# An attention stage on one core: the last two features and the constant column of an outer product move from GpSimd to ScalarE

## The reference, cut to what matters

```python
def _L1_gnn_ref(feat, efeat, W_msg, b_msg, W_attn, b_attn, src, dst):
    w_m = (efeat @ W_msg + b_msg).reshape(E, in_f, -1)
    w_a = (efeat @ W_attn + b_attn).reshape(E, in_f, -1)
    h_src = feat[src][:, :, None]
    e1 = w_m * h_src
    e2 = w_a * h_src
    seg_max = jax.ops.segment_max(e2, dst, num_segments=N)
    ex = jnp.exp(e2 - seg_max[dst])
    denom = jax.ops.segment_sum(ex, dst, num_segments=N)
    attn = ex / denom[dst]
    ft = jax.ops.segment_sum(e1 * attn, dst, num_segments=N)
    return ft.sum(axis=1)
...
x = _layernorm(x + _L0_gnn_ref(x, edge_weight, src, dst), axis=-1)
x = _layernorm(x + _L1_gnn_ref(x, edge_attr_16, L1_gnn_W_msg, L1_gnn_b_msg, L1_gnn_W_attn, L1_gnn_b_attn, src, dst), axis=-1)
x = _layernorm(x + _L2_gnn_ref(x, edge_weight1, L2_gnn_W, L2_gnn_b, src, dst), axis=-1)
x = _layernorm(x + _L3_gnn_ref(x, edge_index, L3_gnn_eps1, ...), axis=-1)
```

## Time and profile before

| | |
|---|---|
| median of three runs | 8206.96 us (8204.55 to 8208.66) |
| the profiled execution | 8196.03 us, of which the traced span is 8194.2 us |
| share of the span: PE, DVE, ACT, POOL | 87%, 85%, 19%, 65% |
| the attention stage: first and last `outer` start | 1295.0 and 4452.2 us |
| granted TensorE clock over the whole span | 0.959 |

### The profile page before, as it was taken

The page is one execution under the profiler, slowest core; times in us unless marked ns, Lnnn a source line. Parts: engine busy times, 40 slices in busy tenths (PEclk is TensorE's granted clock), DMA queues, the critical chain, the costliest instruction groups (busy, mean ns, idle before and its releaser), DMA issues.

```text
span 8194.2 us, 205237 instructions
## 1 busy us (share of the span) xinstructions
PE 7100.0 (87%) x77871; PEld 6660.7 (81%) x77871; DVE 6989.1 (85%) x12224; ACT 1570.8 (19%) x3861; POOL 5336.9 (65%) x4570
## 2 busy tenths in 40 slices
PE   5999985888888988888887099999499997799994
PEld 5999975777777777777776099999499997799994
DVE  7999976999999999999999488888488886688884
ACT  0000002444444444444443200000000000000000
POOL 3555557888888888888886655555455555455554
PEclk9999998999999999999999599999799998899997
DMA  2222213555555455455554211111111111111110
GB/s 88 87 83 87 87 48 91 152 155 155 152 155 156 152 156 154 152 156 155 152 155 145 77 48 46 47 48 46 29 48 48 48 48 32 42 48 47 47 48 21
DMA packets 738221, 757.27 MB, mean 92 GB/s; under 512 B 153760, under 2 KB 698336, under 8 KB 738112
## 3 DMA queue, kind: packets, MB, share of 16 engines
q1 hardware_dynamic: 592640, 667.34, 24.7%
q0 software_dynamic: 140528, 86.77, 6.7%
q10 hardware_dynamic: 5008, 2.59, 0.1%
HBM read 239.80 MB, written 519.73 MB: 93 GB/s over the span
## 4 chain that ended last, share of the span: by engine, by line
PE 41%; DVE 30%; issue 23%; POOL 4%; DMA 1%; DVEq 1%; ACT 0%; ACTq 0%; POOLq 0%; SPq 0%; another core or an unknown queue 0%
PE ps L798 41%; DVE amax_room L1206 6%; DVE spare L1211 4%; DVE flat L1233 3%; DVE msg L1111 2%; DVE stt L928 2%; POOL got L451 2%; DVE flat L928 2%; DVE run L1132 1%; DVE spare L1215 1%; DVE raw L928 1%; DVE wide_buf L928 1%; DVE flat L1090 1%; DVE junk L1138 1%; POOL wide_buf L451 1%
## 5 line engine op out<-in xcount | busy, mean ns | idle before, releaser
L451 POOL DMA_INDIRECT msg<-feat,cidx x1680 | 1686.0, 1004 | 1580.9 <-PE ps L798 1172.2
L798 PE MATMUL ps<-parts,wide_buf 128*128 128x160 bf16 x30240 | 2123.2, 233 | 291.1 <-DVE wide_buf L1090 279.7
L798 PEld LDWEIGHTS ps<-parts,wide_buf 128*128 128x128 bf16 x30240 | 2100.2, 98 | 303.8 <-issue 283.7
L451 POOL DMA_INDIRECT hsrc<-feat,aidx x1568 | 1897.0, 1210 | 457.8 <-issue 327.8
L798 PE MATMUL ps<-parts,flat 128*128 128x160 bf16 x30240 | 2113.3, 233 | 25.7 <-DVE flat L1090 21.1
L798 PEld LDWEIGHTS ps<-parts,flat 128*128 128x128 bf16 x30240 | 2093.6, 98 | 33.1 <-DVE flat L1090 25.1
L845 PEld LDWEIGHTS ps<-wsb,zT 102*128 102x128 f32 x9408 | 1464.1, 190 | 222.9 <-ACT zT L684 201.2
L845 PE MATMUL ps<-wsb,zT 102*128 102x192 f32 (+1 forms) x9408 | 1543.3, 313 | 101.9 <-ACT zT L684 101.2
L1111 DVE TENSOR_REDUCE msg<-raw 128x288 f32<-128x2880 f32 x224 | 1130.4, 5046 | 7.8
L928 DVE TENSOR_TENSOR raw<-ps,amask 128x960 f32<-128x960 f32 x448 | 737.9, 1657 | 463.4 <-PE ps L798 351.0
L451 POOL DMA_INDIRECT msg<-in_x,cidx x560 | 561.3, 1002 | 553.5 <-PE ps L798 310.0
(11 more groups left out here) (218 smaller groups left out, 4681.3 us busy)
## 6 DMA issues: line engine op xcount, KB each, us to landing
state_tab<-flat SPq DMA_DIRECT2D x784, 512.0 KB
raw<-quot_tab SPq DMA_DIRECT2D x224, 576.0 KB
run_tab<-run SPq DMA_DIRECT2D x224, 224.0 KB
top_tab<-spare SPq DMA_DIRECT2D x392, 128.0 KB
msg<-feat,cidx POOLq DMA_INDIRECT x1680
hsrc<-feat,aidx POOLq DMA_INDIRECT x1568
efs<-in_ef SPq DMA_DIRECT2D x392, 34.0 KB
msg<-in_x,cidx POOLq DMA_INDIRECT x560
```

Of the source, the lines that this page charges most:

```text
L451: return pool.indirect_dma_start(dest, None, table, rows_at(idx))
L798: last = nc.tensor.matmul(block.rearrange("p (q c) -> p q c", c=D), hot[s][:, m, t * P:(t + 1) * P], parts[:, m * Q:(m + 1) * Q, part, :], ...
```

## The change

`outer` on GpSimd now makes 14 of the 16 source features (OI = 14) and 16 of the 17 columns: 4 x 14 x 16 = 896 numbers a partition. A new function `fill` on ScalarE makes the rest of `z`, in nine instructions a group: one copies 14 source features of each of the four edges into the constant column (56 numbers), and eight (two features of four edges) copy the 17 edge numbers scaled by one source feature, which is read from `hsrc` as a scalar of each partition. `fill` stands between the two pieces of `turned` and works on the group after TensorE's. The copy of the index list, which stood there, moves behind `weights` piece 0, ahead of `masks`, and is for one group later than before (g + 4 in place of g + 3). A new semaphore pair `a_fill` is waited for by TensorE ahead of a group's first `turn`, by GpSimd's `fetch` ahead of its gathers and by SyncE ahead of the load of `efs`. ScalarE's loop takes four groups a turn where it took two. No other engine's list changes.

```diff
@@ -55,6 +55,7 @@
 CW = CF * F
 HG = G // 2
 TURNS = ((HG, G), (0, HG))
+OI = 14
 assert NB % 2 == 1 and SL < NG // 2 and NB % DC == 0 and K % (2 * G) == 0 and NG % 2 == 0 and 2 * G == 8
 CONT, BOTH, CONT_NEG, BOTH_NEG = range(4)
 
@@ -158,6 +159,8 @@
         hsrc = sb("hsrc", [P, 4, G, D])
         z_room = sb("z_room", [P, 2 * DC * D * F])
         z = z_room[:, 0:2 * G * D * F].rearrange("p (a g c) -> p a g c", a=2, g=G)
+        zs = [z[:, s].rearrange("p g (i f) -> p g i f", f=F) for s in range(2)]
+        ef_rows = [efs[:, s].rearrange("p (g f) -> p g f", f=F) for s in range(2)]
         zT = sb("zT", [P, 3 * G, P])
         wsb = sb("wsb", [P, 3, CF * 2 * D])
         aring = sb("aring", [P, 2, 2, G])
@@ -294,6 +297,7 @@
         a_diff = ring("a_diff")
         s_minus = sem("s_minus")
         a_exp = ring("a_exp")
+        a_fill = ring("a_fill")
         a_egap = ring("a_egap")
         a_w = ring("a_w")
         a_sum = ring("a_sum")
@@ -356,6 +360,7 @@
 
                 def next_ef(j, s):
                     sp.wait_ge(a_z[s], j)
+                    sp.wait_ge(a_fill[s], j)
                     sp.sem_inc(s_sp, 1)
                     load_ef(j, s)
 
@@ -499,6 +504,7 @@
                     pool.wait_ge(a_idx[s], j + 1)
                     if not first:
                         pool.wait_ge(a_z[s], j - 1)
+                        pool.wait_ge(a_fill[s], j - 1)
                     pool.sem_inc(s_pool, 1)
                     for k in range(G):
                         gather(hsrc[:, slot, k, :], feat[1], aidx[:, s, k:k + 1]).then_inc(a_got[s], 16)
@@ -510,9 +516,9 @@
                         pool.wait_ge(a_tr[s], j * G)
                         if paced:
                             pool.wait_ge(a_gap[1 - s], j - 1 + s)
-                    nc.gpsimd.tensor_tensor(z[:, s].rearrange("p g (i f) -> p g i f", f=F),
-                                            efs[:, s].rearrange("p (g f) -> p g f", f=F).unsqueeze(2).to_broadcast([P, G, D, F]),
-                                            hsrc[:, slot].unsqueeze(3).to_broadcast([P, G, D, F]), ALU.mult).then_inc(a_z[s], 1)
+                    nc.gpsimd.tensor_tensor(zs[s][:, :, 0:OI, 0:D], ef_rows[s][:, :, 0:D].unsqueeze(2).to_broadcast([P, G, OI, D]),
+                                            hsrc[:, slot, :, 0:OI].unsqueeze(3).to_broadcast([P, G, OI, D]),
+                                            ALU.mult).then_inc(a_z[s], 1)
 
                 for s in range(2):
                     fetch(0, s, s, True)
@@ -689,6 +695,17 @@
                     act.wait_ge(a_got[s], j * (16 * G))
                 nc.scalar.activation(aidx[:, s, :], sidx[:, bass.ds((2 * j + s) * G, G)], ACT.Copy).then_inc(a_idx[s], 1)
 
+            def fill(j, s, slot, first=False):
+                act.wait_ge(a_ef[s], 16 * (j + 1))
+                act.wait_ge(a_got[s], (j + 1) * (16 * G))
+                if not first:
+                    act.wait_ge(a_tr[s], j * G)
+                last = nc.scalar.activation(zs[s][:, :, 0:OI, D], hsrc[:, slot, :, 0:OI], ACT.Copy)
+                for k in range(G):
+                    for i in range(OI, D):
+                        last = nc.scalar.activation(zs[s][:, k, i, :], ef_rows[s][:, k, :], ACT.Copy, scale=hsrc[:, slot, k, i:i + 1])
+                last.then_inc(a_fill[s], 1)
+
             def weights(j, s, piece):
                 lo, hi = TURNS[piece]
                 act.wait_ge(a_diff[s], 2 * j + piece + 1)
@@ -703,31 +720,39 @@
                     act.wait_ge(a_sum[s], j * G)
                 nc.scalar.activation(aring[:, s], resets[:, :, bass.ds((2 * j + s) * G, G)], ACT.Copy).then_inc(a_ring[s], 1)
 
-            def group(j, s, first=False, ask=True):
+            def group(j, s, half, first=False, ask=True, more=True):
                 b, jb = 1 - s, j - 1 + s
                 turned(j, s, 0)
-                if ask:
-                    indices(j + 1 + s, b)
+                if more:
+                    fill(j + s, b, 2 * ((half + s) % 2) + b)
                 turned(j, s, 1)
                 weights(jb, b, 0)
+                if ask:
+                    indices(j + 2, s)
                 masks(j, s, first)
                 gap_weights(jb, b)
                 weights(jb, b, 1)
 
             for s in range(2):
                 indices(0, s, True)
+            fill(0, 0, 0, True)
             indices(1, 0)
+            fill(0, 1, 1, True)
             for piece in range(2):
                 turned(0, 0, piece)
             masks(0, 0, True)
             indices(1, 1)
-            group(0, 1, True)
-            with act.Fori(1, AHALF - 2) as j:
-                for s in range(2):
-                    group(j, s)
+            indices(2, 0)
+            group(0, 1, 0, True)
+            for s in range(2):
+                group(1, s, 1)
+            with act.Fori(1, AHALF // 2 - 1) as i:
+                for half in range(2):
+                    for s in range(2):
+                        group(2 * i + half, s, half)
             for j in range(AHALF - 2, AHALF):
                 for s in range(2):
-                    group(j, s, ask=2 * j + s + 3 < AG)
+                    group(j, s, j % 2, ask=False, more=2 * j + s + 1 < AG)
             weights(AHALF - 1, 1, 0)
             gap_weights(AHALF - 1, 1)
             weights(AHALF - 1, 1, 1)
@@ -859,6 +884,7 @@
             def group(j, s, first):
                 b, jb = 1 - s, j - 1 + s
                 pe.wait_ge(a_z[s], j + 1)
+                pe.wait_ge(a_fill[s], j + 1)
                 for piece, (lo, hi) in enumerate(TURNS):
                     if not first:
                         pe.wait_ge(a_w[s], 2 * (j - 1) + piece + 1)
```

## The result

The changed kernel takes 8107.66 us (median of four runs, 8100.97 to 8111.31), beside 8205.75 us (8202.72 to 8208.66) for the kernel before: a ratio of 0.988 with a 95% interval of 0.9862 to 0.9897, 98 us less. The forecast was 8091 us with 8070 to 8190 as its range. The profiled execution took 8108.13 us, its traced span is 8106.3.

What follows compares the result with a forecast made beforehand. The prediction took GpSimd, full at 8.04 us a group and stalling VectorE at `rescaled`, to bound the attention stage. 0.30 us over 387 groups gave 8196 - 116 = 8080, plus 11 to the median: 8091 us, range 8070 to 8190.

Steps and rivals of the forecast that it cites:

- The coupling: Attention stage: GpSimd full at 8.04 us a group, its product delaying VectorE's `rescaled` by 0.30; VectorE alone needs 7.74.
- The product: GpSimd's `outer`: from 1,088 to 896 numbers it goes from 2.08 to 1.73 us, a saving of 0.35.
- Fill: ScalarE's nine added instructions: 1.9 us a group, between the pieces of `turned`, costing nothing while under 2.9 us.
- The rival in which ScalarE becomes the bound: Fill of 3.8 us delays `turned`'s second piece and `weighted`: 8362 us; 13% together with other collisions.
- The steady saving: Attention stage: the stall at `rescaled` goes, saving 0.30 us a group over 387 groups, 116 us.
- GpSimd drifts forward until `gap` holds it: GpSimd, 0.06 us a group in hand, moves up to 0.8 us earlier until its product waits for VectorE's `gap`.
- the long pauses stay as they are: GpSimd's 14 stops of some 2 us between gathers, with `rescaled` taking 2.24 behind them, were to stay unchanged.
- VectorE's own pace: Likeliest case: VectorE sets the group at 7.74 us; 8070 to 8110 us, chance 62%.
- a wait of GpSimd for `gap`: Sign of the likeliest case: GpSimd waits for VectorE's `gap` ahead of its product; no size given.

Runs made afterwards that it cites:

- padded kernel: Changed kernel plus a GpSimd write of 224 zeros a partition behind each group's four gathers: 8137.75 us against 8179.86 for the kernel before, ratio 0.9947.
- half product: Changed kernel with GpSimd's product cut to 7 of the 14 features, the others left out: 8047.32 us, ratio 0.9837 to the kernel before.
- fifteenth feature: Changed kernel with fifteen features on GpSimd and one on ScalarE (OI = 15): 8114.32 us, beside 8095.42 for the changed kernel in the same set.
- thirteen: Changed kernel with thirteen features on GpSimd and three on ScalarE (OI = 13): 8074.63 us, beside 8077.64 for the changed kernel in the same set.
- twelve features: Changed kernel with twelve features on GpSimd, four on ScalarE: 8153.19 us, 0.9965; with ScalarE's copies split over two waits: 8111.47 us, 0.9898.
- the copy in front: Changed kernel with the index copy back in its old place, ahead of fill and for group g + 3: 8080.14 us, ratio 0.9877 to the kernel before.
- the copy behind fill: Changed kernel with the index copy for g + 3 behind fill, between the two pieces of `turned`: 8405.86 us, ratio 1.0254 to the kernel before.

## Why the prediction was right, and where it was off

*The coupling.* GpSimd full, VectorE held back by the product beside `rescaled`, VectorE's own group at 7.74: all of it stands. The padded kernel shows that it is GpSimd's whole group that holds, and the half product shows VectorE's 7.75 as the floor. Above that floor the group follows GpSimd's own length one for one: from the kernel before, 8.04 - 0.33 = 7.71 us for the changed one; the zeros add 0.22 to it, the fifteenth feature 0.11, which makes 7.94 and 7.82, and 7.94 and 7.82 were measured.

*The product.* 1.73 was taken, 1.75 came. From 1,088 to 896 numbers it loses 1.70 ns a number, from 896 to 448 (0.96 us in the half product) 1.77. The saving is 0.33 us. The 0.42 us estimated from the Trainium skill (GPSIMD Engine Reference, "Elementwise — side-by-side cycle accounting") would have been too much.

*Fill.* 1.9 us taken, 1.84 measured, with no cost. The eight scaled copies take 1.70 together, 0.2 each. That is close to what the Trainium skill (ScalarE: Activation LUTs, "What ACT_TABLE_LOAD costs") gives for an ACTIVATE with a scalar operand back to back with others. The rival in which ScalarE becomes the bound came true where fill was made 3.4 us long, and not here.

*The steady saving.* Of the 116 us, 387 x (8.04 - 7.75) = 112 arrived. In all 98 us came, 18 fewer than the forecast: 4 are missing here, 12 in the long pauses (below), and 2 lie outside what was followed up.

*The first step that failed: "GpSimd drifts forward until `gap` holds it".* It doesn't. In the changed kernel the product still follows the last gather at once (3010.22 + 1.15, then 3011.39), and the last `gap` before it, one group after the one shown above at 3002.32, had ended at 3010.55, 0.8 us earlier. Where `gap` does hold GpSimd, as in the half product, 0.16 us lie between the two. The place that takes GpSimd's spare time is the first gather, 1.30 us in place of 1.26: it starts at 3005.55, while `rescaled` runs until 3005.99, and ends 0.86 us after that. In the kernel before, `rescaled` ended at 3008.68 and the gather at 3009.54, 0.86 later. So GpSimd is tied to `rescaled`, and all that follows hangs on it. To get away, the gather would have to start before `rescaled` does (3005.30), so GpSimd would have to be quicker by some 0.25 us more; that is an estimate from these rows. With 0.11 more (thirteen) it did not get away, with half a product it did. This step was wrong without harm to the steady group, since VectorE's pace is the floor either way; it matters for the next one.

*The second step that failed, and the missing 12 us: "the long pauses stay as they are".* The stage has 13 of them in either kernel, not 14, and in the changed one they cost more. The earlier trace rows stands behind a delay of another kind, a single one of 1.40 us ahead of the gather at 1407.48, whose cause is not shown; behind the 13 `rescaled` takes the same 2.22 to 2.25. The timeline of one, VectorE and GpSimd:

```profile
1720.93 1.30 POOL L456 DMA_INDIRECT hsrc<-feat,aidx  x1 [0.16 <-issue]
...
1724.40 0.48 DVE L1237 SCALAR_TENSOR_TENSOR spare<-spare,aring,amax_room 128x256 f32<-128x256 f32 x1
1724.54 2.21 POOL L456 DMA_INDIRECT hsrc<-feat,aidx  x1 [2.31 <-issue]
1724.79 0.75 DVE L1259 SCALAR_TENSOR_TENSOR flat<-flat,aring,wide_buf 128x512 f32<-128x512 f32 x1
...
1725.46 0.48 DVE L1241 SCALAR_TENSOR_TENSOR spare<-amax_room,aring,spare 128x256 f32<-128x256 f32 x1
...
1727.06 0.94 POOL L456 DMA_INDIRECT hsrc<-feat,aidx  x1 [0.31 <-issue]
...
1729.27 1.76 POOL L519 TENSOR_TENSOR z_room<-efs,hsrc 128x896 f32<-128x896 f32 x1
1729.43 2.15 DVE L954 TENSOR_TENSOR flat<-stt,wide_buf 128x512 f32<-128x512 f32 x1
...
1737.65 1.50 DVE L954 TENSOR_TENSOR stt<-flat,spare 128x512 f32<-128x512 f32 x1
```

GpSimd pauses for 2.31 us. The gather behind it, at 1724.54, falls among VectorE's instructions with two SBUF inputs and takes 2.21: it ends 0.81 us after `gap` does (1725.94). The product then starts at 1729.27, after `rescaled` and ahead of the first running sum, which takes 2.15 in place of 0.68 (the maximum in the row above). A group later the product is still late and holds `rescaled`, which takes 1.50. VectorE loses 1.47 us at the one and 0.82 at the other. On GpSimd the distance between two products is 2.5 us above the median there, less 0.22 in the two that follow: 2.28, the same loss. In the kernel before it was 1.27, where the product met `rescaled` once, for 2.24 in place of 0.98. With fifteen features the gather behind the pause takes 1.2, the product meets `rescaled` as before, and a pause costs 1.4; so the price goes with what the late product meets. The sum over the stage is 28.8 us against 16.8, with the single delay in the 16.8. That is most of what the forecast is short of: 112 - 12 = 100 us, and the stage is 99.9 us shorter. I had kept the pauses at their old price, though the price is set by the very meeting that the change moves.

*The two profiled executions* differ by 88 us and not 98: the first product starts 5.0 us later in the changed one, and the part behind the last product is 7.0 us longer (3748.9 against 3742.0). In the other traces of the changed kernel the first product starts at 1293.7 and 1293.3, and the part behind is 3728.2 and 3739.0, so this is nothing that the change brings each time.

*The chances.* VectorE's own pace, the likeliest case, is what came. Its range of 8070 to 8110 holds the 8107.66 us by 2 us, and that much was luck: the pauses were priced 12 us too low. Two of the signs given for this case, a wait of GpSimd for `gap` and the drift, did not show.

## To carry to other kernels

Where two engines seem both full, look for the instruction at which one waits inside its own duration: here such a wait was no idle time in any row, only a duration that differed from that of the same form elsewhere (0.98 us for 0.69). Work can be moved to an idle engine for nothing as long as it fits into one wait of that engine and its results are wanted later; the window is read from the engine's idle note and from the time at which the next user needs what is queued behind. Ask of every rare delay what it will collide with after the change: here the same pause cost 1.27 us before it and 2.28 after.

## What the runs showed of the hardware

*GpSimd's product holds VectorE.* An instruction of VectorE with two inputs in SBUF that meets the product ends some 0.56 us after it (`rescaled`: 0.98, 1.50, 2.24, 3.18 us in place of 0.69; the first running sum 2.15). Those with one input in PSUM keep their 0.48 and 0.68 us beside it.

*VectorE holds GpSimd's gather, and not the other way round.* If a two-input instruction of VectorE runs when a gather starts and for some 0.13 us on, the gather ends 0.81 to 0.87 us after that instruction's end. This holds for 1520 of 1536 gathers of the stage before, and for 1484 of 1536 after the change. If none does, the gather takes 0.94 to 0.99 (15 and 39 gathers). That is how 0.95 becomes 1.04, 1.15, 1.26 or 1.42. One gather before and 13 after don't fit (with twelve features 304). The 13 are those behind the long pauses. By the rule the one at 1724.54 would have ended some 0.82 us after 1724.88; it ended 0.81 us after `gap`, two instructions later. In the regular groups a gather doesn't wait for the next two-input instruction, though that has begun before the first one ends. Why it does here is not shown. A gather costs VectorE nothing: running sums beside gathers take the 0.74 us that they take elsewhere.

The Trainium skill (SBUF — State Buffer, "SBUF: two separate sides") tells of an exclusive lock between the two engines, which a VectorE instruction with two SBUF inputs takes against a GpSimd instruction that reads SBUF, and of DMA descriptors that GpSimd can't write until VectorE is done. The traces agree that one is blocked wholly, and they show the wait of a gather for two-input instructions too. They differ in two points. The page lets whichever starts first keep the lock; in the earlier trace rows `rescaled` had begun 0.54 us before the product and was held all the same, as far as the recorded starts can tell. And it gives about 115 ns from VectorE's end, where these gathers need 0.81 to 0.87 us to their own end.

*An index copy and its gather.* A gather starts 0.81 us after the end of the copy that it waits for, if nothing else holds it: in 322 of 345 groups with the copy in front, and from 3008.53 to 3009.34 with the copy behind fill.

*The long pauses.* From the second one on, every 112 gathers, in the kernel before and in the changed one, GpSimd pauses for 2.0 or 2.3 us between two of them. What it does there is not in the trace, and no run here shows it.
